# Attention scores activated three PSUM banks at a time instead of two, in an attention-and-FFN block on one core

## The reference

```python
xp = silu(x @ W1 + b1)                      # x [1, 2048, 128], W1 [128, 512]
u, v, q, k = split(xp, 4)                   # 16 heads of 8 features each
scores = einsum('bqhd,bkhd->bhqk', q, k)
attn = silu(scores) / S                     # no softmax
av = einsum('bhqk,bkhd->bqhd', attn, v)
x = layernorm(x + layernorm(av * u, gamma, beta) @ W2 + b2)
# FFN with rows and weights rounded to blockwise FP4 (blocks of 16), then fp32 matmuls
x = layernorm(x + fp4_linear(silu(fp4_linear(x, w_gate)) * fp4_linear(x, w_up), w_down))
```

## Time and profile before

| what | value |
|---|---|
| median of 3 runs (lowest, highest) | 515.42 us (514.72, 517.13) |
| the profiled execution's own time | 514.83 us |
| its span, first to last instruction | 513.0 us |
| mean granted TensorE clock | 0.998 |
| PE busy, ACT busy | 495.9 us (97%), 487.4 us (95%) |
| PEld busy, DVE busy, POOL busy | 263.9 us, 281.4 us, 56.9 us |

### The profile page before, as it was taken

One profiled execution on the slowest core, in us unless ns is written; L12 is line 12 of the kernel. 1 busy time (PEld: TensorE's weight loads), 2 busy tenths in 40 slices (PEclk: granted clock), 3 DMA queues, 4 the chain that ended last, 5 costly groups with the idle time before them and its releaser, 6 DMA issues.

```text
span 513.0 us, 20141 instructions
## 1 busy us (share of the span) xinstructions
PE 495.9 (97%) x9030; PEld 263.9 (51%) x9032; DVE 281.4 (55%) x738; ACT 487.4 (95%) x548; POOL 56.9 (11%) x148
## 2 busy tenths in 40 slices
PE   9899999999999999999999999999999999999996
PEld 5443344444353444434354444434477777777762
DVE  6546642755748475665847475574343443544445
ACT  5999999999999999999999999999999999999940
POOL 7620000001010100101010100101010101101010
PEclk9999999999999999999999999999999999999999
DMA  7932340000000000000000000000000000000000
GB/s 190 231 85 60 96 134 3 1 3 7 3 6 3 8 2 3 6 1 8 3 7 3 8 1 3 6 4 6 3 8 4 9 4 10 9 3 9 4 3 12
DMA packets 15156, 12.39 MB, mean 24 GB/s; under 512 B 1783, under 2 KB 14718, under 8 KB 15070
## 3 DMA queue, kind: packets, MB, share of 16 engines
q1 hardware_dynamic: 14088, 9.44, 7.5%
q0 software_dynamic: 688, 1.40, 1.1%
q10 hardware_dynamic: 294, 0.26, 0.2%
HBM read 1.92 MB, written 1.05 MB: 6 GB/s over the span
## 4 chain that ended last, share of the span: by engine, by line
ACT 51%; PE 31%; issue 15%; DVE 2%; POOL 0%; POOLq 0%; DVEq 0%
ACT attn L643 50%; PE ps L405 29%; PE ps L419 2%; PE ps L448 1%; ACT v_sb L643 0%; POOL rstd_b L388 0%; DVE xn_b L769 0%; DVE stats_b L799 0%; ACT feat L643 0%; DVE xn_b L777 0%; DVE xn_b L773 0%; DVE xn_b L775 0%; POOLq L141 0%; DVE magic_b L771 0%; POOL ve_b L387 0%
## 5 line engine op out<-in xcount | busy, mean ns | idle before, releaser
L643 ACT ACTIVATE attn<-ps 128x1024 f32<-128x1024 f32 x512 | 475.8, 1211 | 0.3 <-PE ps L405 0.2
L405 PE MATMUL ps<-attn,v_pad 128*32 128x256 f32 (+1 forms) x5120 | 274.4, 341 | 0.3 <-DVE wdown_t L979 0.2
L405 PE MATMUL ps<-q_stack,k_stack 64*128 64x256 bf16 (+1 forms) x2560 | 173.6, 251 | 10.4 <-ACT attn L643 1.5
L405 PEld LDWEIGHTS ps<-attn,v_pad 128*32 128x32 f32 x5120 | 132.2, 109 | 80.2 <-issue 39.6
L405 PEld LDWEIGHTS ps<-q_stack,k_stack 64*128 64x128 bf16 x2560 | 78.6, 94 | 133.5 <-ACT attn L643 87.1
L387 POOL TENSOR_TENSOR ve_a<-mv_a,eps_col 128x1 f32<-128x1 f32 x24 | 4.6, 191 | 230.2 <-DVE mv_a L801 230.2
L387 POOL TENSOR_TENSOR ve_b<-mv_b,eps_col 128x1 f32<-128x1 f32 x24 | 4.6, 191 | 202.7 <-DVE mv_b L801 202.7
L742 DVE CAST parts<-feat 128x512 bf16<-128x512 f32 (+1 forms) x10 | 3.8, 383 | 25.3 <-ACT feat L643 25.3
L405 PE MATMUL ps<-zeros 128*128 128x512 bf16 x46 | 12.2, 412 | 1.4 <-DVE zeros L916 1.2
L388 POOL TENSOR_TENSOR rstd_a<-ve_a,minus_half 128x1 f32<-128x1 f32 x24 | 13.3, 555 | 1.9
L388 POOL TENSOR_TENSOR rstd_b<-ve_b,minus_half 128x1 f32<-128x1 f32 x24 | 13.3, 555 | 1.9
(11 more groups left out here) (183 smaller groups left out, 405.6 us busy)
## 6 DMA issues: line engine op xcount, KB each, us to landing
q_stack<-parts SPq DMA_DIRECT2D x18, 128.0 KB, 2.4
k_stack<-parts SPq DMA_DIRECT2D x15, 128.0 KB, 3.8
x_sb<-in_L_attn_x SPq DMA_DIRECT2D x3, 256.0 KB, 5.1
k_stack<-zeros SPq DMA_DIRECT2D x6, 128.0 KB, 5.4
q_stack<-zeros SPq DMA_DIRECT2D x6, 128.0 KB, 2.4
k_stack<-parts SPq DMA_DIRECT2D x9, 64.0 KB, 2.7
q_stack<-parts SPq DMA_DIRECT2D x9, 64.0 KB, 2.0
out<-x_a SPq DMA_DIRECT2D x8, 64.0 KB, 1.5
```

The costliest lines, as they stand in the source:

```text
L405: return pe.matmul(to, lhsT, rhs, start=start, stop=stop, skip_group_check=True)
L643: return act.activation(to, frm, ACT.Silu, **kw)
```

## The change

The scores of the chunks of 256 are grouped anew. A piece is now a quarter of a step: one head set in both halves of rows, 256 columns for each half. Six pieces (a step and a half) have twelve such half pieces, and make two groups of three banks, 1536 columns each, activated by one instruction of 128x1536. The two groups use banks 0 to 2 and banks 3 to 5, in turn, so TensorE may fill a group's banks when the activation two groups before has ended. There are 256 such groups in place of 384.

A bank is still written from one half of the rows only. With three banks to a group, the first group has four half pieces of rows 0 to 63 (banks 0 and 2) and two of rows 64 to 127 (bank 1); the second has two and four. `by_turns` issues them two at a time; the third two of a group are of the same half of rows and go to the same bank.

`times_v` goes by half steps (4 matmuls) and is issued for the half steps whose groups lie at least two back: one half step behind one group, two behind the next. Jobs follow the half step that the planned step would have followed. The chunks of 128 keep groups of two banks, three in turn, and two half steps of `times_v` behind every second group. `attn` keeps its size (12 x 512 columns), and `av_done` counts half steps.

```diff
-    RING = 3
-    SB = 3
+    PIECES = 4 * len(STEPS)
+    THREES = 4 * BEGIN[sum(w == 256 for w in WIDTHS)]
+    GROUPS = []
+    for p in range(0, THREES, 6):
+        n = len(GROUPS)
+        GROUPS.append((0, 3, n % 4 * 3 * CH, ((p, 0, 0), (p, 1, 512), (p + 1, 0, 256), (p + 1, 1, 768),
+                                              (p + 2, 0, 1024), (p + 3, 0, 1280))))
+        GROUPS.append((3, 3, (n + 1) % 4 * 3 * CH, ((p + 4, 0, 512), (p + 2, 1, 0), (p + 5, 0, 768), (p + 3, 1, 256),
+                                                    (p + 4, 1, 1024), (p + 5, 1, 1280))))
+    TWOS = len(GROUPS)
+    for p in range(THREES, PIECES, 2):
+        n = len(GROUPS) - TWOS
+        GROUPS.append((n % 3 * 2, 2, n % 6 * 2 * CH, ((p, 0, 0), (p, 1, 512), (p + 1, 0, 256), (p + 1, 1, 768))))
+    SUMMED = [sum(last_group(h) <= n - 2 for h in range(THREES // 2)) for n in range(TWOS)]
+    for n in range(TWOS, len(GROUPS), 2):
+        SUMMED += [SUMMED[-1], THREES // 2 + n - TWOS + 2 - 2 * LAG]
...
+            def scores(n):
+                first_bank, banks, _, some = GROUPS[n]
+                if same_banks(n):
+                    pe.wait_ge(attn_ready, same_banks(n))
...
+                for k in range(0, len(some), 2):
+                    for p, half, col, m, b, a in by_turns(some[k:k + 2]):
...
+                        last = mm(ps[:, bank, to:to + w], k_stack[rows, M * b + m, i * P:(i + 1) * P],
+                                  q_stack[rows, M * b + m, Q0[c]:Q0[c] + w])
...
+            def times_v(h):
...
+                pe.wait_ge(attn_ready, last_group(h) + 1)
+                for p in (2 * h, 2 * h + 1):
...
+            for n in range(len(GROUPS)):
+                scores(n)
+                for h in range(SUMMED[n - 1] if n else 0, SUMMED[n]):
+                    times_v(h)
+                if n in JOB_BEHIND:
+                    job(JOB_BEHIND[n])
...
+            for n, (bank, banks, first, _) in enumerate(GROUPS):
+                act.wait_ge(scores_ready, n + 1)
+                if same_columns(n):
+                    act.wait_ge(av_done, same_columns(n))
+                silu(attn[:, first:first + banks * CH], ps[:, bank:bank + banks, :]).then_inc(attn_ready, 1)
```

More of the change, by code:

```diff
@@ L94, in group @@
         return [(m, b) for m in some[a * len(some) // 2:(a + 1) * len(some) // 2] for b in range(2)]
+    PIECES = 4 * len(STEPS)
+    THREES = 4 * BEGIN[sum(w == 256 for w in WIDTHS)]
+    ATTN = 12 * CH
+    assert THREES % 6 == 0
+    GROUPS = []
[5 more added lines that the diff above has]
+                                                    (p + 4, 1, 1024), (p + 5, 1, 1280))))
@@ new lines, in build, with heads, last_group @@
+    TWOS = len(GROUPS)
+    for p in range(THREES, PIECES, 2):
+        n = len(GROUPS) - TWOS
+        GROUPS.append((n % 3 * 2, 2, n % 6 * 2 * CH, ((p, 0, 0), (p, 1, 512), (p + 1, 0, 256), (p + 1, 1, 768))))
+    PLACE = {(p, half): (n, first + col) for n, (_, _, first, some) in enumerate(GROUPS) for p, half, col in some}
+    def heads(p):
+        c, g, _ = STEPS[p // 4]
+        some = group(c, g, p % 4 // 2)
+        return some[p % 2 * len(some) // 2:(p % 2 + 1) * len(some) // 2]
+    def last_group(h):
+        return max(PLACE[p, half][0] for p in (2 * h, 2 * h + 1) for half in range(2))
@@ new lines, in build, with same_banks, banks, same_columns @@
+    SUMMED = [sum(last_group(h) <= n - 2 for h in range(THREES // 2)) for n in range(TWOS)]
+    for n in range(TWOS, len(GROUPS), 2):
+        SUMMED += [SUMMED[-1], THREES // 2 + n - TWOS + 2 - 2 * LAG]
+    def same_banks(n):
+        def banks(k):
+            return range(GROUPS[k][0], GROUPS[k][0] + GROUPS[k][1])
+        return max((k + 1 for k in range(max(n - 4, 0), n) if set(banks(k)) & set(banks(n))), default=0)
+    def same_columns(n):
+        def columns_of(k):
+            return range(GROUPS[k][2], GROUPS[k][2] + GROUPS[k][1] * CH)
+        before = [k for k in range(max(n - 8, 0), n) if set(columns_of(k)) & set(columns_of(n))]
+        return max((p // 2 + 1 for k in before for p, _, _ in GROUPS[k][3]), default=0)
@@ L96, in build, with group_of_job @@
+    def group_of_job(at):
+        if at < LAG:
+            return last_group(2 * at + 1)
+        return next(n for n in range(len(GROUPS)) if SUMMED[n] >= 2 * (at - LAG) + 2)
     AV = [6 + c % 2 for c in range(len(WIDTHS))]
     def spare_bank(at):
+        assert at < LAG or STEPS[(SUMMED[group_of_job(at)] - 1) // 2][0] == STEPS[at - LAG][0]
         return 13 - AV[STEPS[at - LAG][0]] if at >= LAG else 7
@@ L127, in build @@
     JOB_BANK = [spare_bank(at) for at in sorted(JOB_AT)]
+    JOB_BEHIND = {group_of_job(at): at for at in JOB_AT}
+    assert len(JOB_BEHIND) == len(JOB_AT)
     job_no = {job: k for k, job in enumerate(JOBS)}
@@ L191, in build @@
         q_stack = sb("q_stack", [P, SLOTS, S], BF16)
-        attn = sb("attn", [P, RING, 2, 2, CH])
+        attn = sb("attn", [P, ATTN])
         zu = sb("zu", [P, CH])
@@ L475, in wait_stacked, with by_turns @@
                     wait_stack(pe, unit_no[("q", Q0[c])])
-            def scores(at):
+            def by_turns(two):
+                for j in range(len(heads(two[0][0]))):
+                    for p, half, col in two:
+                        yield p, half, col, *heads(p)[j], j * WIDTHS[STEPS[p // 4][0]]
+            def scores(n):
+                first_bank, banks, _, some = GROUPS[n]
+                if same_banks(n):
+                    pe.wait_ge(attn_ready, same_banks(n))
+                else:
+                    pe.wait_ge(head_act, max(head_last[first_bank + i] for i in range(banks)) + 1)
+                for k in range(0, len(some), 2):
+                    for p, half, col, m, b, a in by_turns(some[k:k + 2]):
+                        c, g, i = STEPS[p // 4]
+                        w = WIDTHS[c]
+                        if p % 4 == half == a == 0:
+                            wait_stacked(c, g, i)
+                        rows = slice(64 * half, 64 * half + 64)
+                        bank, to = first_bank + (col + a) // CH, (col + a) % CH
+                        last = mm(ps[:, bank, to:to + w], k_stack[rows, M * b + m, i * P:(i + 1) * P],
+                                  q_stack[rows, M * b + m, Q0[c]:Q0[c] + w])
+                last.then_inc(scores_ready, 1)
@@ L478, in scores @@
+            def times_v(h):
+                at = h // 2
                 c, g, i = STEPS[at]
                 w = WIDTHS[c]
[L480 to L499, removed]
+                if h % 2 == 0 and c == g == 0 and i % TPC == 0:
                     pe.wait_ge(v_padded, i // TPC + 1)
-                if g == i == 0:
+                if h % 2 == g == i == 0:
                     wait_spare(AV[c], at + LAG)
-                for a in range(2):
-                    pe.wait_ge(attn_ready, 2 * at + a + 1)
-                    for k, (m, b) in enumerate(group(c, g, a)):
+                pe.wait_ge(attn_ready, last_group(h) + 1)
@@ L506, in times_v @@
+                for p in (2 * h, 2 * h + 1):
+                    for k, (m, b) in enumerate(heads(p)):
                         for half in range(2):
                             cols = slice(32 * (2 * half + b), 32 * (2 * half + b) + 32)
-                            last = mm(ps[cols, AV[c], 0:w], v_pad[:, i, m, cols],
-                                      attn[:, at % RING, a, half, k * w:(k + 1) * w],
+                            a = PLACE[p, half][1] + k * w
+                            last = mm(ps[cols, AV[c], 0:w], v_pad[:, i, m, cols], attn[:, a:a + w],
@@ L595, in behind @@
                 return down_of(r, bank, 0)
[L597 to L604, removed]
+            for n in range(len(GROUPS)):
[4 more added lines that the diff above has]
+                    job(JOB_BEHIND[n])
+            for h in range(SUMMED[-1], 2 * len(STEPS)):
+                times_v(h)
             def keep_warm(piece):
@@ L691, in job @@
                     silu(ROWS[tile % 2].gate[:, :], ps[:, JOB_BANK[k], 0:FF]).then_inc(job_by_act, 1)
[L693 to L702, removed]
+            for n, (bank, banks, first, _) in enumerate(GROUPS):
[3 more added lines that the diff above has]
+                silu(attn[:, first:first + banks * CH], ps[:, bank:bank + banks, :]).then_inc(attn_ready, 1)
+                if n - 1 in JOB_BEHIND:
+                    job(JOB_BEHIND[n - 1])
             r = TAIL_ROWS
@@ L790, in take_av @@
                 w = WIDTHS[c]
-                dve.wait_ge(av_done, BEGIN[c + 1])
+                dve.wait_ge(av_done, 2 * BEGIN[c + 1])
                 for tile in range(TAIL):
```

## The result

The changed kernel takes 538.67 us (median of 4 runs, 538.38 to 542.63), the kernel before 516.21 (4 runs, the three of the table above among them): a ratio of 1.0455, with a 95% interval of 1.0425 to 1.0485. It is slower by 22.5 us. The forecast was 537.5 us, range 529 to 549. The profiled execution took 538.73 us.

What follows compares the result with a forecast made beforehand. TensorE was to become the bound: scores 138.2, times v 198.1 and jobs 41.9 make 378.2 us, plus 3.0 of waits 381.2, 22.2 over 359.0. Added to 514.83 that is 537.0, or 537.6 on the median's footing; forecast 537.5, range 529 to 549.

Steps and rivals of the forecast that it cites:

- Bound before: Wide stage before: ScalarE slightly slower than TensorE, which needs 335.6 of 359.0 us and has 23.4 us of room.
- pieces of 6.17 us: Wide stage's chain before: once in every chunk an unbroken 6.17 us all TensorE, where "down" and "y" fall on neighbouring steps.
- The fourth round: Wide scores: a three-bank group takes 0.54 us, as a step did; 256 groups against 192 steps add 34.6 us.
- Times v in 254 blocks: Wide times v: alternating blocks of four (0.56 us) and eight (1.00 us) take 198.1 us, 8.1 more than before.
- Jobs at nothing: Jobs in the wide stage keep instructions and order, so moving them from steps to groups costs nothing extra.
- Waits, 3.0 us: Wide stage with two groups in turn: TensorE waits 1.8 us at the start and 1.2 in the first chunk.
- 1.2 us for ScalarE's share of jobs: First chunk: ScalarE's share of a job can hold back a bank; 1.2 us allowed of its 11.9.
- The sign named for the waits: Profile after: TensorE's waits for activations should fall from 204 to the start and the first chunk.
- Rival 1: Wide scores: two matmuls in one half cost no extra round, ScalarE stays the bound, 509 to 514 us; chance 0.10.
- Rival 2: Wide stage: ScalarE's job work and stalls, 11.9 us, come on top of TensorE's work, 546 us; chance 0.07.
- Rival 3: Wide scores: the last matmul's weight load is not hidden, 94 ns more per group, 561 us; chance 0.05.
- an estimated 6.4 us: ScalarE in the wide stage: 128 fewer activation starts of about 0.05 us offer a gain of 6.4 us.

Runs made afterwards that it cites:

- e4: Kernel before, but in wide steps each of the two groups of scores is followed by half of times v (four matmuls): 542.50 us, ratio 1.0518.
- e1: Changed kernel, but the last scores matmul of each three-bank group works on the other half of the rows, its own half piece not computed: 517.84 us, ratio 1.0047.
- e5: Kernel before, but each wide group's four scores matmuls are issued first, first, second, second half of the rows instead of in turn: 515.87 us, ratio 0.9991.
- e8: Changed kernel, but from the fifth group on ScalarE activates only two of the three banks of each wide group: 539.96 us, ratio 1.0471.
- e2: Changed kernel, but times v is issued only behind every second group, twelve matmuls at a time, some jobs moved: 541.88 us, ratio 1.0504.
- e3: Changed kernel with the edits of both e1 and e2: 530.98 us, ratio 1.0309.
- e6: Changed kernel regrouped into wide groups of four and two banks in turn, filled evenly from both row halves, everything computed: 524.56 us, ratio 1.0169.
- e7: As e6, but times v in twelves behind the groups of four and jobs behind the groups of two: 530.26 us, ratio 1.0299.
- e9: Changed kernel with the edits of both e1 and e8: 511.77 us, ratio 0.9909.

## Why the prediction was right

*Bound before.* Two nearly level engines, TensorE with 23.4 us of room in the wide stage. e4 bears this out: 46 us of TensorE's work were added to the kernel before and the stage grew by 25.5, so about 20 were taken up. One reading of the chain was wrong: pieces of 6.17 us that are all TensorE stand in its wide stage nine times, 29.3 us apart, so once for each tile of 128 rows and not once in each of six chunks. No term of the sum used their number. Two of the nine:

```profile
110.47 6.17 PE ps L405 x116
...
139.80 6.17 PE ps L405 x116
```

*The fourth round, 64 x 0.54 = 34.6 us more for scores.* Shown: 0.54 for six matmuls, and 0.43 when one moves to the other half (e1). The reason given was too narrow. It is not that the two matmuls are neighbours (e5) but that one half has four of the six.

*Times v in 254 blocks, 8.1 us more.* A block of four was to take 0.56 and takes 0.57. e4 shows the price without anything else of the change: 0.24 us for each alternation, part of it on the scores' side. Counted by cause, the change adds 256 rounds (256 x 0.11 = 28 us) and 64 alternations (64 x 0.24 = 15 us), 43 us against 23.4 of room, where the prediction had 42.7 in the same two terms.

*Jobs at nothing.* They cost TensorE what they cost before (0.70 from "gate" to the next scores, at 132.21 and 132.91), and VectorE was busy for the same 210 us.

*Waits, 3.0 us.* The start is visible in the timeline of the changed kernel: 1.32 us for an activation and 0.27 for k_stack, 1.6 where 1.8 was set for k_stack alone:

```profile
16.71 0.39 PE L463 MATMUL ps<-q_stack,k_stack 64*128 64x256 bf16 x4 [1.32 <-ACT attn L708]
17.37 0.39 PE L463 MATMUL ps<-q_stack,k_stack 64*128 64x256 bf16 x2 [0.27 <-DMA k_stack<-parts]
```

The 1.2 us for ScalarE's share of jobs are not seen: the matmuls of the stage wait for activations twice, 1.6 us in all, and 1.32 of it are the wait at the start. The stage is 4.4 us over the work as priced; 1.6 are these waits at the start and 1.3 the blocks of four, and 1.5 stay unassigned. That the total comes so close to the forecast is in part luck.

The sign named for the waits did not come out as written. They should have shrunk to the start and the first chunk, and 64 of the 77 lie behind 76 us. None of these 64 is over 0.6 us, while the weight loads of the scores are idle for 0.41 us before them (0.57 behind a job) even where they wait for nothing, so hardly any of them cost time.

The stage was forecast at 381.2 us and is 382.6; everything behind it took what it took before, and the time before it is 0.3 us longer (14.56 against 14.28).

*The rivals.* Rival 1, no round of its own for the last two, fell with the 0.54. Its price would have been wrong too: e1 has the rounds of that case, and it is 0.5% slower than before, not 509 to 514 us. The prediction took too little for level engines here. Rival 2, both costs add, did not hold in the changed kernel (e8). Where TensorE's work was made smaller, in e1, e2, e3, e6 and e7, the stage ran 13 to 42 us over it; e9 shows for e1 that ScalarE has a part in this, and for the others the share of each cause is not shown. Rival 3, weights not hidden, is refuted by the loads of the group at 130.78 in the changed kernel:

```profile
130.78 0.33 PEld L463 LDWEIGHTS ps<-q_stack,k_stack 64*128 64x128 bf16 x6 [0.41 <-issue]
```

All six loads are over 0.33 us after the start. The last of them takes 0.09 and so began at about 0.24, beside the fifth matmul, which started at 0.23 in the same half. The rule of the Trainium skill (TensorE: Matmul & The Clock Gate, Part 3, "The mechanism"), that a load overlaps matmuls in flight only in another row group, does not hold for this form; by it the time would have been 561 us. The same section also lets a load pass when it goes to a background weight buffer, and these rows agree with that.

## What to carry to other kernels

When matmuls use half of the array's rows, count how many fall in each half within a run of one array shape: in the orders tried here the fuller half set the rounds. Price an engine that shows 97% busy by the distances between the starts of its blocks, and count how often it alternates between array shapes, because each alternation is paid (0.24 us here). And a larger group in the same memory means fewer groups in turn. It saves starts on the engine that reads, here an estimated 6.4 us; e1, which has that saving and no fourth round, was still no faster than the kernel before.

## What the runs showed of the hardware

Order within a run did not matter: four matmuls issued as first, first, second, second half of the rows took two rounds (e5: eight in 0.55 us, four pairs), as in turn. Six matmuls with four in one half took four rounds, 0.54 us, and with three in each half three, 0.43. A weight load of 0.09 us ran beside a matmul in the same half of the rows. Going once more from one array shape to the other and back took 0.24 us (e4). And one ACTIVATE over three PSUM banks costs its columns plus the same start as over two: 1.33 us for 1536 columns against 0.904 for 1024, 0.43 for 512 more.
